# A sequential gated memory between two expert layers: keys of the last chunk stay as they are, and the first state meets the queries in one column

## The reference, cut to what matters

```python
c0 = jnp.zeros((Bs, H, HD, HD)); n0 = jnp.ones((Bs, H, HD)); m0 = jnp.zeros((Bs, H))
def step(carry, inp):
    c, n, m = carry
    qt, kt, vt, it, ft = inp
    m_t = jnp.maximum(ft + m, it)
    ie, fe = jnp.exp(it - m_t), jnp.exp(ft - m_t + m)
    c = fe * c + ie * einsum('bhd,bhe->bhde', vt, kt)
    n = fe * n + ie * kt
    num = einsum('bhde,bhe->bhd', c, qt)
    den = jnp.maximum(jnp.sum(n * qt, -1, keepdims=True), 1.0)
    return (c, n, m_t), num / den
```

## Time and profile before

| | us |
|---|---|
| median of three runs | 448.0 |
| span of the profiled execution | 448.0 |
| first expert layer and the way to the first sequence | about 0 to 123.5 |
| first, second and third sequence | 123.5 to 187.8, 187.9 to 252.2, 252.2 to 316.5 |
| fourth sequence with the early routing, and the second expert layer | 316.5 to 448.0 |

### The profile page before, as it was taken

One profiled execution on the slowest core, in us unless ns is written; L12 is line 12 of the kernel. 1 busy time (PEld: TensorE's weight loads), 2 busy tenths in 40 slices (PEclk: granted clock), 3 DMA queues, 4 the chain that ended last, 5 costly groups with the idle time before them and its releaser, 6 DMA issues.

```text
span 448.0 us, 11432 instructions
## 1 busy us (share of the span) xinstructions
PE 383.7 (86%) x3623; PEld 302.6 (68%) x3645; DVE 342.7 (77%) x1061; ACT 225.4 (50%) x591; POOL 125.8 (28%) x125
## 2 busy tenths in 40 slices
PE   8166999999998899898899898899888967879991
PEld 5022999945876677776668676678667843669991
DVE  4883577766649989869989689999699997658870
ACT  3731444425465565455584455475555641455650
POOL 5574244511003101111110121111021138544552
PEclk9669899999999999999999999999999987999996
DMA  7996122159999999999500000000000612333320
GB/s 217 368 411 177 39 72 71 54 147 168 168 166 158 169 162 166 153 150 159 102 1 0 0 0 0 0 0 0 1 1 1 233 53 83 108 99 91 88 78 2
DMA packets 57265, 46.11 MB, mean 103 GB/s; under 512 B 4111, under 2 KB 53905, under 8 KB 56721
## 3 DMA queue, kind: packets, MB, share of 16 engines
q1 hardware_dynamic: 53618, 37.84, 41.8%
q0 software_dynamic: 2752, 5.73, 3.7%
q10 hardware_dynamic: 864, 2.15, 1.6%
HBM read 17.99 MB, written 27.25 MB: 101 GB/s over the span
## 4 chain that ended last, share of the span: by engine, by line
issue 41%; PE 23%; DVE 18%; POOL 9%; ACT 3%; DMA 3%; DVEq 1%; POOLq 0%; SPq 0%; another core or an unknown queue 0%; ACTq 0%
PE bank L896 21%; POOL HS L567 5%; POOL slots L519 3%; PE bank L1033 1%; DVE ST L1419 1%; ACT WVT L786 1%; ACT E L795 1%; POOL LA L561 1%; DMA XN<-slots 1%; DVE W1R L2006 1%; DVE OUT L2044 1%; DVE W1R L2008 1%; DVE W1R L2005 1%; DMA QKT<-by_token 1%; DMA slots<-XN,POS 1%
## 5 line engine op out<-in xcount | busy, mean ns | idle before, releaser
L567 POOL TENSOR_TENSOR HS<-HS,MHALF 128x8 f32<-128x8 f32 x16 | 26.3, 1646 | 148.2 <-DVE HS L1999 148.2
L786 ACT ACTIVATE WVT<-bank,AC 128x128 f32<-128x128 f32 x128 | 36.6, 376 | 29.0 <-PE bank L896 29.0
L896 PE MATMUL bank<-XBT,W1R 128*128 128x128 f32 x368 | 50.6, 282 | 0.2 <-ACT XBT L689 0.2
L896 PE MATMUL bank<-W,HT 128*128 x368 | 49.0, 276 | 1.6 <-issue 1.6
L896 PEld LDWEIGHTS bank<-XBT,W1R 128*128 128x128 f32 x368 | 45.8, 196 | 1.0 <-ACT XBT L689 0.6
L896 PEld LDWEIGHTS bank<-W,HT 128*128 128x128 f32 x368 | 44.8, 192 | 2.3 <-issue 2.0
L696 ACT ACTIVATE HT<-bank,W1R 128x128 f32<-128x128 f32 x115 | 34.8, 366 | 16.6 <-PE bank L896 10.9
L896 PE MATMUL bank<-MASKB,IDB 128*128 128x512 bf16 x130 | 35.6, 400 | 4.9 <-POOL HS L567 3.2
L519 POOL DMA_INDIRECT slots<-XN,POS x32 | 32.2, 1006 | 18.7 <-issue 8.7
L750 ACT ACTIVATE QKT<-bank,COLS 128x512 f32<-128x512 f32 x32 | 22.0, 687 | 26.5 <-PE bank L896 26.5
L1953 DVE TENSOR_TENSOR WOT<-bank,WVT 128x512 f32<-128x512 f32 x32 | 21.9, 685 | 14.7 <-ACT WVT L786 14.7
(11 more groups left out here) (360 smaller groups left out, 983.6 us busy)
## 6 DMA issues: line engine op xcount, KB each, us to landing
slots<-FILL SPq DMA_DIRECT2D x74, 258.0 KB
W<-w SPq DMA_DIRECT2D x2, 2048.0 KB, 10.6
XN<-slots SPq DMA_DIRECT2D x23, 129.0 KB
W<-w SPq DMA_DIRECT2D x1, 2064.0 KB
slots<-QKT SPq DMA_DIRECT2D x1, 1483.5 KB, 6.8
XB<-slots SPq DMA_DIRECT2D x23, 64.5 KB
X<-x SPq DMA_DIRECT2D x4, 256.0 KB, 5.3
QKT<-by_token SPq DMA_DIRECT2D x4, 256.0 KB, 4.1
```

The source lines that it names most:

```text
L567: g.tensor_tensor(HS[:, 3, :], HS[:, 2, :], MHALF[:, 0:H], ALU.pow).then_inc(roots_ready, 1)
L786: ins = a.activation(DT[:, hf, m, :], DM[:, m * P:(m + 1) * P], ACT.Exp, bias=AC[:, c, h:h + 1])
L896: return t_.matmul(o, l, r, start=start, stop=stop, skip_group_check=True)
```

## The change

Four edits. The use "k3" is taken out of `TR_USES`, and with it the turning of the last chunk's keys (on TensorE) and their weighing (on VectorE) for each of the 4 sequences. `state_decays` and `head_gates` of the last chunk stay where they are. In `to_state` the wait for the reading of "k{c}" is dropped; the wait of `tr_wait` for the use just ahead of "u{c}" covers it, which an assertion states. And `from_state` of a sequence's first chunk multiplies the queries with the 65th column of the state alone, not with all 65.

```diff
-        TR_USES = ["k0", "k1", "u0", "k2", "u1", "o0", "d0", "k3", "u2", "o1", "d1", "o2", "d2", "o3", "d3"]
+        TR_USES = ["k0", "k1", "u0", "k2", "u1", "o0", "d0", "u2", "o1", "d1", "o2", "d2", "o3", "d3"]
@@ from_state (TensorE)
+                first = HD if c == 0 else 0
                 for m in range(4):
                     for hf in range(2):
                         rows = slice(hf * HD, (hf + 1) * HD)
 
                         for half in [slice(0, P)] if m == 0 else [slice(0, HD), slice(HD, P)]:
-                            mm(NB_[hf][half, m * 65:(m + 1) * 65], QS[rows, m, half], CS[rows, m, :], m == 0, False)
+                            mm(NB_[hf][half, m * 65 + first:(m + 1) * 65], QS[rows, m, half], CS[rows, m, first:],
+                               m == 0, False)
@@ to_state (TensorE)
                 pe.wait_ge(*pj_read_at(b, f"v{c}"))
-                pe.wait_ge(*tr_read_at(b, f"k{c}"))
+
+                assert TR_USES.index(f"u{c}") > TR_USES.index(f"k{c}")
                 dst = tr_wait(b, f"u{c}")
@@ chunk (TensorE)
-                if more:
+                if c < NC - 2:
                     k_tokens(b, c + 1)
-                elif not last:
+                if not more and not last:
                     state_decays(b, c)
                     head_gates(b + 1)
```

## The result

| | before | changed |
|---|---|---|
| median of the first runs, us | 446.8 (six, 445.3 to 449.1) | 441.6 (six, 440.4 to 445.5) |
| ratio to before | 1 | 0.9887, 95% interval 0.9839 to 0.9936 |
| profiled execution: run, span, us | span 448.0 | run 445.5, span 443.2 |

One run of before in a later round, 488.3 us at a granted clock of 0.74 where the others have 0.94 to 0.97, was in a slower state and is in no ratio.

The account below looks back on a forecast made before the run. In chunk c = 2, TensorE's stall delays ScalarE's exponentials E, which set QS's start, with VectorE's queue close behind. 448.0 less 2.82 us (3 x 0.68 + 0.78, other edits 0) gives 445.2 us; range 443.2 to 448.2.

Parts of the forecast that it names:

- Edit one: Last chunk's keys removed: QS in chunk c = 2 starts 0.68 us earlier in three sequences, 0.78 in the fourth; 2.82 us.
- Both bounds of the sum: Four sequences' gain from removing the keys: 2.4 us from VectorE's 0.61 slot, 3.3 from GpSimd's 0.83 limit, per sequence.
- the cap of 0.83: Chunk c = 2: GpSimd's root, ending at 220.33 and not moving, limits the path's gain to 0.83 us per sequence.
- The two rivals about its size: TensorE's whole stall comes back (440.3 us; full or above cap, chance 0.06), or the gain is absorbed (448.0 us, 0.10).
- later of two: Chunk c = 2: QS starts at the later of VectorE's queue, 219.16, and E's end plus 0.02 us, 219.27.
- Edit two: `from_state`, first chunk: one column in place of 65 in 4 x 28 instructions saves 0, hidden behind VectorE.
- Edit three: Dropped wait in `to_state`: implied by the bank's order, worth one sequencer step, 0; no new wait arises.
- period 63.6: Sign in the changed profile: QS to the next sequence's same QS is 63.6 us apart instead of 64.3.
- The base: Starting time of 448.0 us, taken as both profiled span and median of the runs, without correction.
- The clock behind the last sequence: First expert blocks: PE's clock comes back late, 1.9 us more per block, 452.8 us from four blocks; chance 0.04.
- the sign of being wrong: Expert blocks: a PE clock below 1.00 there in the changed profile would show the forecast wrong.

Follow-up runs that it names:

- e6: Kernel before, the last chunk's keys still turned on TensorE but read by VectorE in 8 columns of 512: 446.1 us in one run.
- e7: Changed kernel with a 128x512 product kept on VectorE in the removed one's place, nothing on TensorE: 445.2 us in its one run.
- e3: Kernel before with the one-column products alone: 446.5 us, ratio 0.9983.
- e2: Kernel before, all keys' work kept, last chunk's keys on their own semaphores so the bank counts 14; wait in `to_state` left out: 444.5 us, ratio 0.9962.
- e1: Kernel before with the last chunk's keys neither turned nor weighed, bank's count kept at 15, 65 columns kept: 442.2 us, ratio 0.9932.
- e14: Repeat of the kernel before with the count of 14 and all the keys' work kept: 442.7 us.
- e5: Changed kernel again, no edit, for a second trace: 441.4 us, ratio 0.9890.
- e11: Changed kernel again, no edit, for a third trace: 442.1 us, ratio 0.9875.
- e12: Repeat of the changed kernel with 65 columns throughout: 442.0 us, ratio 0.9862.
- e4: Changed kernel with 65 columns throughout in place of the one-column products: 442.6 us, ratio 0.9949.

## Why the prediction was wrong in size

- **Edit one (2.82 us).** Right in mechanism and close in size: E right behind the copy of "o", 0.72 us in each looped sequence for 0.68, 0.85 in the fourth for 0.78, together 3.0 us. Both bounds of the sum, 2.4 and 3.3, hold, though the fourth sequence went past the cap of 0.83, which was read in the second. E came 0.47 us behind the start of the copy of "o", where 0.52 was taken. The two rivals about its size fell: the period is neither 62.5 (64.3 less 1.9 is 62.4) nor 64.3. e6 and e7 show the "later of two" that it rested on.
- **Edit two (0).** Right: e3 moved no distance outside the stretch with the fallen clock, and the 28 loads took 0.76 for "about 0.81".
- **Edit three (0), the step that failed.** "No time falls to it but one sequencer step, 0" looked at the waits in `to_state` and "u2" and not at the list `TR_USES`, whose length is the step of every wait on the bank in the loop. That length fell from 15 to 14, where two other pairs of counters already stood, and 11 register instructions of VectorE (12 of TensorE, 3 of ScalarE) went with it. Measured with e2 alone: 0.41 us at each turn inside the loop, 1.1 from first to last root and about 1.3 in all, and 0 in e1, which holds the count. The wait in `to_state` itself was rightly put at 0: no joint that changed is at it. A hint was in the earlier trace rows, "0.19 <-DVE UB" in front of CS: UB was VectorE's own instruction ahead, and in e2 the same pair follows in 0.72 us with no idle time marked. The "period 63.6" of the forecast came out as 63.20 in the changed kernel and as 63.58 in e1, where the count was held.
- **The base (448.0).** "The profiled span and the median of the runs are both 448.0, so no correction is made" was wrong twice. A run's time is the span and some 2 us more (445.5 for a span of 443.2; 451.2 for 449.1; 445.4 for 443.6; 1.8 to 3.1 over all runs), so the profiled execution of before was one of about 450 us, an estimate. And the median of three was 1.2 above that of six, 446.8 (446.8 over 54 as well). By 446.8 the same terms would have given 444.0, and with the missed 1.3 it is 442.7. Of the 6.4 us between 448.0 and 441.6, 2.8 were forecast, 0.2 are edit one's size, 1.3 the count and 1.2 the base; about 0.9 are left.
- **The clock behind the last sequence (slower rival).** The first expert blocks ran at a lower clock in one of four executions of the changed kernel, but in three of four of before, so it didn't come with the change, and the sign of being wrong that the prediction names (a clock below 1.00 there) can't tell. Another stretch with a fallen clock, which the forecast doesn't have, lies inside the fourth sequence, costs 0.8 to 1.0 us, and took something off the gain where it came.
- **Small slips in the numbers.** 444.7 and 445.6 with 1.5 us either way give 443.2 and 447.1, not 443.3 and 447.2. In the fourth sequence E was taken at 1.15 us where its row has 1.20; with that the term is 0.73 in place of 0.78, and 0.85 came.
- **What stays open.** Root to root the gain is 4.1 us where the clock holds and 3.1 to 3.3 where it falls, and about 0.25 comes ahead of the first root. Over the runs timed in rounds the medians are 446.8 (54) and 441.5 (18), 5.3 us apart. The end, from the last root on, averages 71.7 us in the four executions of before and 70.5 in the four of the changed kernel; no end of the one four lies among those of the other, but two executions of the same kernel differ there by up to 3.0 us (e2 and e14), so that 1.1 us may or may not belong to the change. The way to the first root (139.2 to 145.2 us) varies still more. No experiment here tells the remaining 1 us (2 where the clock falls) apart from chance, and it isn't counted as shown.

## What to carry to other kernels

In a hand-synchronised loop, a wait's target is computed from the pass number and the number of events in a pass, and in this program each distinct step brought register instructions with it on the engines that wait. When an edit takes an event out of a list, cost the new step for the whole loop and not only the waits that are rewritten. A short idle time put down to the engine's own last instruction can be such an instruction. Compare two traces by the distances of one recurring instruction: here they repeat to 0.06 us, but for the stretch with the fallen clock, while the spans differ by 4.5, and an edit with effects at two places shows as two distances.

## What the runs showed of the hardware

- **Instructions without a row cost time.** Eleven written-out register instructions fewer on VectorE, with fewer on two other engines, gave 0.41 us a pass, in four steps of 0.08 to 0.16, but the remaining 90 taken away gave only 0.2 more. The reading is that it counts where they stand: at the four joints one stood behind a wait on the path that sets the pace. That the others run while the engine has work or waits anyway is argued, not shown.
- **The clock may fall or not in the same program.** Over some 7 us around the first root of the fourth sequence, TensorE's granted clock was at 0.76 to 0.85 in three of four executions of the changed kernel, in one of two of the same with 65 columns, and in the one of e3, and at 1.00 in the other executions, those of before among them. With it, 228.6 us from first to last root become 229.4 to 229.6. Some 0.5 of that comes after the clock is back at 1.00: in e5 QS of c = 1 waits 0.53 us for E, and in e11, without the fall, it doesn't wait. What decides between the two isn't settled: not the columns (e12), and by e4 and e12 not the program alone.
- **Few columns cost a matmul nearly what many do.** 28 fp32 starts with 65 moving columns take 0.81 us (29 ns each), with one column 0.76 (27 ns); it is 0.81 in each sequence of before and 0.76 in each looped c = 0 with one column.
